# Host-laid-out inputs, an output stored turned and new engine orders in an attention and FFN kernel

## The reference

```python
x = L0_attn_resid_stream                         # (8, 256, 128) f32
xn = _layernorm(x, axis=-1)
x = x + _L0_attn_ref(xn, ...) + _L0_ffn_ref(xn, ...)
# attention, with a = _layernorm(xn, ln_w, ln_b)
q = einsum('bsd,hde->bshe', a, W_q) + b_q        # k, v alike
scores = where(causal, einsum('bqhe,bkhe->bhqk', q, k) * D_HEAD ** -0.5, -inf)
z = einsum('bhqk,bkhe->bqhe', softmax(scores, axis=-1), v)
attn_out = einsum('bqhe,hed->bqd', z, W_o) + b_o
# FFN
_quantize(W) = clip(round(W / (mean(abs(W)) + EPS)), -1.0, 1.0)
h = relu(einsum('bsd,fd->bsf', x, _quantize(W1)) + b1)
out = einsum('bsf,df->bsd', h, _quantize(W2)) + b2
```

## Time and profile before

| | |
|---|---|
| median of 3 runs (lowest, highest) | 269.41 us (269.0, 269.49) |
| profiled execution: its own time, its span | 270.71 us, 268.7 us |
| PE matmul busy | 259.7 us, 97% |
| PE weight load busy | 226.8 us, 84% |
| DVE busy | 233.4 us, 87% |
| ACT busy | 222.8 us, 83% |
| POOL busy | 212.0 us, 79% |
| granted TensorE clock | 1.000 throughout |

### The profile page before, as it was taken

How to read it: one execution, slowest core, us unless ns; L and a number is a source line. 1 busy time by engine, 2 the same in 40 slices (tenths; PEclk the granted TensorE clock), 3 DMA queues, 4 the chain that set the end, 5 groups by cost and what they waited for, 6 DMA issues and landing times.

```text
span 268.7 us, 7430 instructions
## 1 busy us (share of the span) xinstructions
PE 259.7 (97%) x2420; PEld 226.8 (84%) x2420; DVE 233.4 (87%) x1006; ACT 222.8 (83%) x798; POOL 212.0 (79%) x431
## 2 busy tenths in 40 slices
PE   6989899999999999999999999999999999999994
PEld 5767688799888998899897998889887998989874
DVE  2799999998999899997999899998999979997841
ACT  3589997988888997988978988889969889996950
POOL 5489999999859979599768979599786997576750
PEclk9999999999999999999999999999999999999999
DMA  7980000000000000000000000000000000000000
GB/s 166 257 206 1 1 2 4 0 1 2 22 1 2 0 23 1 4 0 2 20 4 4 0 2 20 4 2 2 20 2 1 2 1 22 0 4 0 22 2 20
DMA packets 12737, 5.72 MB, mean 21 GB/s; under 512 B 6790, under 2 KB 12444, under 8 KB 12700
## 3 DMA queue, kind: packets, MB, share of 16 engines
q1 hardware_dynamic: 12656, 5.25, 8.1%
q10 hardware_dynamic: 44, 0.01, 0.0%
HBM read 4.21 MB, written 1.05 MB: 20 GB/s over the span
## 4 chain that ended last, share of the span: by engine, by line
PE 87%; DVE 4%; POOL 3%; ACT 2%; DMA 1%; issue 0%; SPq 0%; POOLq 0%; ACTq 0%
PE m_ps L846 11%; PE s_ps L812 11%; PE m_ps L825 6%; PE m_ps L787 6%; PE m_ps L850 5%; PE m_ps L832 5%; PE m_ps L826 5%; PE m_ps L788 5%; PE m_ps L789 5%; PE s_ps L817 5%; PE m_ps L873 3%; PE m_ps L799 3%; PE m_ps L800 2%; PE m_ps L801 2%; DMA wq_raw<-in_L_attn_W_q 1%; PE m_ps L877 1%
## 5 line engine op out<-in xcount | busy, mean ns | idle before, releaser
L604 DVE CUSTOM_DVE_ANT_0 s_ps<-s_ps,causal 128x256 f32<-128x256 f32 (+1 forms) x256 | 84.8, 379 | 0.0
L465 ACT ACTIVATE prob<-s_ps,neg_max 128x256 f32<-128x256 f32 x128 | 65.4, 511 | 8.4 <-DVE neg_max L604 8.4
L384 POOL TENSOR_SCALAR prob<-prob,inv_sum 128x128 f32<-128x128 f32 x128 | 48.4, 378 | 24.1 <-DVE inv_sum L611 24.1
L386 POOL TENSOR_SCALAR prob<-prob,inv_sum 128x256 f32<-128x256 f32 x128 | 61.8, 483 | 0.0
L467 ACT ACTIVATE prob<-s_ps,neg_max 128x128 f32<-128x128 f32 x128 | 52.3, 409 | 0.0
L473 ACT ACTIVATE pT_wide<-m_ps 128x512 f32<-128x512 f32 x64 | 38.6, 606 | 16.2 <-PE m_ps L826 16.0
L377 POOL TENSOR_TENSOR qk_first<-k_all 128x128 f32<-128x128 f32 x64 | 29.1, 461 | 14.8 <-DVE k_all L592 14.7
L812 PE MATMUL s_ps<-k_all,q_last 64*128 64x256 f32 x384 | 39.2, 310 | 0.3 <-ACT prob L467 0.3
L846 PE MATMUL m_ps<-pT_wide,v 128*64 128x256 f32 x256 | 39.3, 385 | 0.0
L604 DVE DVE_READ_ACCUMULATOR2_ANT neg_max<- 128x1 f32 x256 | 36.2, 141 | 0.0
L812 PEld LDWEIGHTS s_ps<-k_all,q_last 64*128 64x128 f32 x384 | 26.9, 185 | 9.3 <-issue 7.7
...
## 6 DMA issues: line engine op xcount, KB each, us to landing
...
```

Of the source, the lines that this page charges most:

```text
L384: nc.gpsimd.tensor_scalar(prob[:, j, h, S:W], prob[:, j, h, S:W], inv_sum[:, j, 2 + h:3 + h], 0.0, ALU.mult, ALU.add)
L386: last = nc.gpsimd.tensor_scalar(prob[:, j, h, 0:S], prob[:, j, h, 0:S], inv_sum[:, j, h:h + 1], 0.0, ALU.mult, ALU.add)
L465: nc.scalar.activation(prob[:, j, h, 0:S], s_ps[:, pair % 2, h, 0:S], ACT.Exp, bias=neg_max[:, j, h:h + 1], scale=-1.0, accum_out=row_sum[ ...
L604: last = nc.vector.tensor_tensor_reduce(out=sc, in0=sc, in1=mask, scale=-SCALE, scalar=-MASKED, op0=ALU.add, op1=ALU.min, accum_out=neg_ma ...
```

## The change

The host now lays out what the kernel had to rearrange:

- W_q, W_k, W_v come as (128, 1024), feature by head and e, so a row is contiguous; W_o, W1 and W2 come as they lie in SBUF, W1 and W2 turned. Steps tf and cf are gone.
- All vectors of length 128 come as the columns of one (128, 24) array, loaded by one DMA on ACT's queue; L730, vc and vd are gone, as are five small DMAs on ACT's queue and two on SP's. POOL's bo (the sum of b_o and b2, L428) is now POOL's first step.
- The residual comes a second time, turned (8, 128, 256), into a tile with two slots, loaded two batches ahead by SP; DVE adds output bias and turned residual in one operation and the output is stored turned, from two slots. Steps ot, on PE and on DVE, are gone. The host turns the result back.
- The first halves of W_q and W_k are loaded, and split into high and low parts, in quarters of 256 columns; pr0 waits for the low parts of q and k one by one.
- The filler transposes are 12 and 5 instead of 4, 9 and 9.
- All twelve lists are new. The scores of pair 0 and the heads of duo 0 of the next batch are taken into the body's list; the body starts at tw4 of the batch before.

```diff
-BUSY = (4, 9, 9)
+BUSY = (12, 5)
+PARTS = [("q", slice(0, 2 * P)), ("k", slice(0, 2 * P)), ("q", slice(2 * P, 4 * P)), ("k", slice(2 * P, 4 * P)),
+         ("v", HALF[0]), ("q", HALF[1]), ("k", HALF[1]), ("v", HALF[1])]
-PE_HEAD = ("xa:3 xb:1 vd:1 pr0:2 pr1:0 pr2:3 xn:2 s0 pr3:0 s1 v0:2 v1:1 tf0:2 tf1:3 ta:0 s2 pr4:1 pr5:3 v2:2 s3 "
-           "tw0:0 pr6:1 pr7:2 f0:0 s4 tw1:3 v3:0 tn0:1 xh+:2 s5 f1:0 xn+:1 s6 tw2:3 pr0+:2 pr1+:1 s7 tw3:0 "
-           "pr2+:3 pr3+:2 tn1:1")
-PE_PLAN = ("z0-:0 z1-:1 s0 s1 tw4-:2 v0:3 tw5-:0 tn2-:1 tw6-:2 pr4:3 tw7-:0 tn3-:1 pr5:2 v1:0 s2 z2-:1 z3-:3 s3 "
-           "s4 tw0:2 v2:0 tw1:1 pr6:2 pr7:0 v3:1 oa-:3 f0:1 xh+:2 f1:0 s5 s6 tw2:2 tn0:1 xn+:0 ob- pr0+:2 pr1+:1 "
-           "ot-:0 tw3:3 s7 pr2+:2 pr3+:3 tn1:1")
+PE_HEAD = ("xa:0 xb:1 pr0:3 pr1:1 xn:3 pr2:2 pr3:1 s0 pr4:3 s1 ta:0 s2 v0:1 pr5:0 pr6:2 pr7:3 s3 s4 v1:1 v2:2 "
+           "v3:0 xh+:3 tw0:1 tw1:2 pr0+:3 f0:2 f1:1 s5 s6 tn0:2 pr1+:1 xn+:3 pr2+:2 pr3+:1 tw2:0 tw3:3 s7 s0+ "
+           "z0:0 tn1:2")
+PE_PLAN = ("tw4-:1 pr4:3 tn2-:2 z1-:1 s1 s2 tw5-:3 tw6-:2 tn3-:0 v0:1 tw7-:3 pr5:0 pr6:2 pr7:3 z2-:1 z3-:0 s3 s4 "
+           "v1:1 v2:2 v3:0 xh+:3 tw0:1 tw1:2 oa-:0 pr0+:3 f0:2 f1:1 s5 s6 tn0:2 pr1+:1 xn+:3 ob- pr2+:2 pr3+:1 "
+           "tw2:0 tw3:3 s7 s0+ z0:0 tn1:2")
+PE_TAIL = ("tw4-:3 pr4:1 tn2-:2 tw5-:3 z1-:0 s1 s2 tw6-:2 tn3-:0 pr5:1 tw7-:3 v0:0 pr6:2 pr7:3 v1:0 s3 z2-:1 "
+           "z3-:2 s4 s5 oa-:1 f0:2 ob- tw0:0 f1:2 tn0:3 tw1:1 s6 s7 tw2:2 tw3:0 tn1:3 v2:1 tw4:2 v3:0 tw5:3 z0:1 "
+           "z1:2 tw6:0 tn2:1 tn3:3 tw7:0 z2:1 z3:2 oa:3 ob")
...
+ACT_HEAD = ("wh0 wh1 wh2 xa wh3 wh4 pr0 pr1 xn pr2 pr3 aa wh5 e0 oh pr4 e1 e2 e3 pr5 pr6 pr7 e4 e5 e6 xh+ w0 e7")
+ACT_PLAN = ("w1- e8- e9- pr0 f0- f1- e10- pr1 e11- xn e12- pr2 e13- w2- w3- pr3 e14- z0- e15- w4- e0 pr4 e1 z1- "
+            "w5- w6- e2 e3 w7- pr5 pr6 pr7 e4 e5 z2- z3- e6 xh+ w0 e7")
...
+DVE_HEAD = ("lz nh wl0 wl1 wl2 xb wl3 xl pr0 pr1 xn pr2 pr3 m0 m1 th te0 te1 pr4 m2 i0 m3 m4 ln+ v0 pr5 m5 i1 pr6 "
+            "pr7 m6 i2 v1 v2 v3 m7 xh+ m8 m9 pr0+ m10 i3 m11 n0 m12 i4 pr1+ xn+ m13 pr2+ i5 i6 m14 m15 pr3+ m0+ "
+            "n1 z0 m1+ i7 n2 pr4+ z1 m2+ i0+ m3+ n3")
+DVE_PLAN = ("m4 ln+ v0 pr5 m5 i1 pr6 pr7 z2- m6 i2 z3- v1 v2 v3 m7 xh+ m8 m9 pr0+ m10 i3 m11 n0 m12 i4 pr1+ xn+ "
+            "o- m13 pr2+ i5 i6 m14 m15 pr3+ m0+ n1 z0 m1+ i7 n2 pr4+ z1 m2+ i0+ m3+ n3")
...
+POOL_HEAD = ("bo hs np vl0 g0 g1 k0 k1 k2 k3 vl1 ol p0 k4")
+POOL_PLAN = ("ln p1- xl k5- k6- p2- h0- k7- p3- k0 h1- k1 p4- p5- p6- k2 k3 p7- p0 k4")
+POOL_TAIL = ("ln p1- k5- k6- xl k7- p2- k0 p3- p4- k1 h0- p5- p6- k2 p7- k3 k4 h1- k5 p0 p1 p2 k6 p3 p4 k7 h0 p5 "
+             "h1 p6 p7")
...
             sp.dma_start(x_all[:, 0:TILES, :], x_v[:, 0:TILES, :]).then_inc(x_in[0], 16)
-            for n, w in (("q", w_q), ("k", w_k), ("v", w_v)):
-                load_half(n, w, 0)
+            for n in range(5):
+                load_weights(n)
             sp.dma_start(x_all[:, TILES:2 * TILES, :], x_v[:, TILES:2 * TILES, :]).then_inc(x_in[1], 16)
...
+            load_turned(0)
+            load_turned(1)
             for b in range(B):
-                sp.wait_ge(ot_done, b + 1)
-                sp.dma_start(out_v[b], out_sb[:, :, :]).then_inc(out_done, 16)
-            sp.wait_ge(out_done, 16 * B)
+                sp.wait_ge(o_done, b + 1)
+                sp.dma_start(outT[b], out_sb[:, b % 2, :]).then_inc(out_done[b % 2], 16)
+                if b + 2 < B:
+                    load_turned(b + 2)
...
+            act.dma_start(vecs[:, :], columns).then_inc(vec_in, 16)
...
                 wait(dve, o_psd, b + 1)
-                nc.vector.tensor_scalar(o_part[:, :], bank("oa", 0, b)[:, 0:S], out_bias[:, :], None, ALU.add).then_inc(o_done, 1)
+                dve.wait_ge(xT_in[b % 2], 16 * (b // 2 + 1))
+                wait(dve, out_done[b % 2], 16 * (b // 2))
+                nc.vector.scalar_tensor_tensor(out=out_sb[:, b % 2, :], in0=bank("oa", 0, b)[:, 0:S],
+                                               scalar=out_bias[:, :], in1=xT_cur[:, b % 2, :], op0=ALU.add, op1=ALU.add)\
+                    .then_inc(o_done, 1)
```

More of the change, by code:

```diff
@@ L51 @@
[L51 to L63, removed]
@@ new lines @@
+ACT_HEAD = ("wh0 wh1 wh2 xa wh3 wh4 pr0 pr1 xn pr2 pr3 aa wh5 e0 oh pr4 e1 e2 e3 pr5 pr6 pr7 e4 e5 e6 xh+ w0 e7")
+ACT_PLAN = ("w1- e8- e9- pr0 f0- f1- e10- pr1 e11- xn e12- pr2 e13- w2- w3- pr3 e14- z0- e15- w4- e0 pr4 e1 z1- "
+            "w5- w6- e2 e3 w7- pr5 pr6 pr7 e4 e5 z2- z3- e6 xh+ w0 e7")
+ACT_TAIL = ("w1- e8- e9- pr0 f0- f1- e10- pr1 xn e11- e12- pr2 e13- w2- pr3 w3- e14- e15- z0- w4- e0 pr4 e1 z1- "
+            "w5- e2 w6- w7- pr5 e3 pr6 e4 e5 e6 z2- e7 z3- e8 pr7 e9 e10 f0 e11 w0 f1 w1 w2 w3 e12 e13 w4 e14 e15 "
+            "z0 w5 z1 w6 w7 z2 z3")
@@ new lines @@
+DVE_HEAD = ("lz nh wl0 wl1 wl2 xb wl3 xl pr0 pr1 xn pr2 pr3 m0 m1 th te0 te1 pr4 m2 i0 m3 m4 ln+ v0 pr5 m5 i1 pr6 "
[3 more added lines that the diff above has]
+            "o- m13 pr2+ i5 i6 m14 m15 pr3+ m0+ n1 z0 m1+ i7 n2 pr4+ z1 m2+ i0+ m3+ n3")
+DVE_TAIL = ("m4 m5 v0 pr5 i1 pr6 m6 v1 m7 z2- i2 m8 m9 m10 z3- i3 pr7 i4 m11 o- n0 i5 m12 m13 n1 v2 m14 i6 m15 v3 "
+            "i7 z0 n2 z1 n3 z2 z3 o")
@@ L105, with attention_ffn_kernel @@
 BEFORE = before_it()
-def attention_ffn_kernel(nc, resid, attn_mask, w_q, w_k, w_v, w_o, b_q, b_k, b_v, b_o, ln_w, ln_b,
-                         w1, b1, w2, b2, out):
+def attention_ffn_kernel(nc, x, xT, w_q, w_k, w_v, w_o, w1T_in, w2T_in, columns, b_v, outT):
     ctx = ExitStack()
@@ L279, in _, with load_weights @@
         def _(sp):
[L280 to L285, removed]
+            x_v = x.rearrange("b (t p) d -> p (b t) d", p=P)
+            def load_weights(n):
+                name, cols = PARTS[n]
+                sp.dma_start(raw[name][:, cols], {"q": w_q, "k": w_k, "v": w_v}[name][:, cols]).then_inc(w_in[n], 16)
@@ L309, in _ @@
+            for n in range(2):
+                sp.wait_ge(out_done[n], 16 * B // 2)
         @block.gpsimd
@@ L779, in project @@
                     wait_low_input(b)
-                if b == 0 and pair < PAIRS // 2:
+                if b == 0 and 0 < pair < PAIRS // 2:
                     pe.wait_ge(w_lo_done, 2 + 2 * (pair // 2))
@@ L786, in project @@
                     dst = halves("pr", pair, b)[:, n, :]
+                    if b == 0 and pair == 0:
+                        pe.wait_ge(w_lo_done, n + 1)
                     nc.tensor.matmul(dst, wlo[kind][:, cols], x2T_hi[:, :], start=True, stop=False)
@@ L888, in last_output @@
                 last.then_inc(o_psd, 1)
-            def turn_output(b):
-                wait(pe, o_done, b + 1)
-                for t in range(TILES):
-                    last = nc.tensor.transpose(bank("ot", 0, b)[:, t * P:t * P + P], o_part[:, t * P:t * P + P], ident[:, :])
-                last.then_inc(ot_psd, 1)
             def turn_first_heads_input(kind):
@@ L916, in turn_hidden_input @@
                 last.then_inc(xn_psd, 1)
-            def turn_ffn(n):
-                pe.wait_ge(w12_in, 32)
-                for c in range(FC):
-                    src = w2_raw[:, c * P:c * P + P] if n else w1_raw[:, c, :]
-                    last = nc.tensor.transpose(bank("tf", n, 0)[:, c * P:c * P + P], src, ident[:, :])
-                last.then_inc(wT_psd, 1)
             def total_ffn():
@@ L970, with laid_out, by_input @@
         "L0_ffn_W1", "L0_ffn_b1", "L0_ffn_W2", "L0_ffn_b2"]
+def laid_out(x, _, w_q, w_k, w_v, w_o, b_q, b_k, b_v, b_o, ln_w, ln_b, w1, b1, w2, b2):
+    def by_input(w):
+        return w.transpose(1, 0, 2).reshape(D, H * E)
+    columns = np.stack([*b_q.reshape(PAIRS, P), *b_k.reshape(PAIRS, P), *b1.reshape(FC, P), ln_w, ln_b, b_o, b2], axis=1)
+    return {"x": x, "xT": x.transpose(0, 2, 1), "w_q": by_input(w_q), "w_k": by_input(w_k), "w_v": by_input(w_v),
+            "w_o": w_o.reshape(PAIRS, P, D).transpose(1, 0, 2).reshape(P, PAIRS * D), "w1T": w1.T,
+            "w2T": w2.T.reshape(FC, P, D).transpose(1, 0, 2).reshape(P, FC * D), "columns": columns,
+            "b_v": b_v.reshape(1, H * E)}
 def kernel(**inputs):
```

160 lines of the change are left out of this document (44 added, 116 removed).

## The result

The changed kernel takes 283.32 us (median of 4 runs, 282.79 to 283.79), the kernel before 269.45 beside it (269.00 to 270.02): a ratio of 1.0513, 95% interval 1.0482 to 1.0544. Its profiled execution took 283.72 us with a span of 281.8. The forecast was 269.8, the range 264.5 to 272.0: wrong.

A forecast was written before the change was run, and what follows sets the result against it. TensorE's stream bounds the body, and what feeds it the first batch. First batch 44.0 + six batches 184.4 + last batch 37.5 + waiting 0.2 + end 3.0 = 269.1 span, 269.8 us as a median; range 264.5 to 272.

The forecast's parts named there:

- Start: Before the first projection: turned input ready at 7.5 us, projection starting at 7.55 instead of 9.07, a gain of 1.5.
- the walk: First batch, followed step by step through the engines with start distances: PE leaves it at 44.4 us, taken as 44.0.
- Order of the first batch: First batch in the body's order with nothing ready: PE leaves it at 44.0 us, the least being 38.4.
- Period: Length of one batch in the body: 30.74 us instead of 31.01, bounds 30.5 to 30.9; six make 184.4.
- the output turn's 0.22: Every batch: two transposes of the output go from PE, saving 0.22 us.
- Last batch and end: Last batch 37.5 us plus 0.2 of waiting; behind the last matmul 3.0 instead of 4.05.
- the span plus 0.7: Whole kernel: the median of the runs was taken as the profiled span plus 0.7 us.
- A: Rival, first batch: it keeps its pace of 38.4 us, so the median is 264.2; chance 0.29.
- B: Rival, first batch: DVE's ternaries collide with POOL's wo_lo, losing up to 1.4 us, so 271.2; chance 0.20.
- the 1.49 row: Profile of the kernel before, near 8.25 us: a DVE subtraction took 1.49 us instead of 0.41 while POOL's wv_lo ran.
- C: Rival, body: the loop of DVE and ACT sets the period, 31.2 us, and all is 272.6; chance 0.11.
- D: Host's layout: changes nothing by itself, loads being hidden but for the first 5 us; part of the forecast, no separate chance.

The follow-up runs named there:

- e1: The changed kernel, with projection 0 of the first batch no longer waiting for the late halves of the weights: 276.48 us, ratio 1.0251.
- e2: e1 with POOL's wo_lo moved later in the first batch, away from DVE's ternaries: 275.45 us, ratio 1.0194.
- e9: e1 with POOL's first narrow keys ahead of the late halves, wo_lo and smaller steps moved, and PE's second scores ahead of a projection: 274.16 us, ratio 1.0185.
- e5: The changed kernel's layout and turned output without pair 0's late wait, but engine lists of the kernel before, less removed steps: 268.47 us, ratio 0.9953.

## Why the prediction was wrong

*The step that failed* is "Start", with its "x2T_lo at 7.5, pr0 at 7.55. Gain 1.5", and behind it the walk that begins with it. x2T_lo ended at 7.84, nearly as said; pr0 started at 14.32. I priced the waits that the change takes away from pr0 and never asked which waits are left once its condition is changed: pair 0 moved to the `elif`, and that waits for POOL. The walk then had DVE take pr0 at 9.55. That wait, which the prediction put at nothing, cost 6.8 us (e1).

*Order of the first batch*: 44.0 against 56.12, 12.1 too little. The runs split it, each by tw4 of one profiled execution, with the difference of the medians behind it: 6.8 the wait (e1; 6.8); 1.4 the collision with wo_lo (e2 against e1; 1.0, within the noise); 2.0 the late halves ahead of k0, pr4 ahead of s1 and the smaller moves beside them (e9 against e2, 48.00 to 46.03; 1.3). The last 2.0, to 44.0, no run isolates; e9 has at most half of it in its collision (1.53 for 0.48), and its clock was 0.59 and 0.73 from 15 to 25 us. I had walked DVE and ACT step by step and taken POOL, whose new list puts 3.8 us of late halves ahead of k0, as "close behind". That was the second fault: the walk checked POOL at its divisions, not at k0.

*Start, once the wait is gone*: 7.98 in e1 and 7.86 in e5, a gain of 1.1 to 1.2 for 1.5. The columns' DMA, for which I took nothing, did cost nothing: POOL waited 0.63 for it, had done bo by 2.97, and then waited 1.19 more for DVE. Its first rstd starts at 4.16 for 3.92 before, because DVE's statistics, which wait for the input's load, start at 3.11 for 2.87. And little of the gain reaches the body: with the old orders (e5) the whole first batch is about 0.2 shorter in the medians.

*Period*: 30.85 for 30.74, inside 30.5 to 30.9. The hole from s3 to s4 is gone (0.60 for 0.74). But the output turn's 0.22 is no saving by itself: with the old orders it buys nothing at all, since ACT sets the length from pr0 to pr3 there (e5). So what I summed term by term is one joint result of turn and orders.

*Last batch and end*: from 56.12 + 6 x 30.85 = 241.2 to the last matmul at 278.86 is 37.6 for 37.7; 3.0 for 3.0 behind it. Both right.

*From the span to the median.* The terms together are 12.7 too low (281.8 for 269.1); the other 0.8 of the 13.5 is the step "the span plus 0.7". It set the median of some executions against the span of another, slower one. The changed kernel's median is 1.5 above its profiled span, and a profiled execution's own time 1.9 above it (283.72 for 281.8).

*Rivals.* A is wrong: even with wait, late halves and wo_lo mended the new first batch is at 46.03, not 38.4. B happened, with 1.98 us for my 1.4 in the operation and 1.4 at tw4 (1.0 in the medians); I gave it 0.20 though the 1.49 row showed it beside POOL's like operation. C is wrong for the new orders: the period is 30.85 and not 31.2. D isn't contradicted: with the old orders the layout and the turned output together are 0.5% faster, but nearly all of that is the end, which the turned output shortens. About 0.2 us is left for the rest, no more than the noise.

The range had no case for the first batch above 46, while the walk was the least certain term. A term built from some 60 ordered steps deserved a bound of several us upward; a new order has many ways to be late and one to be on time.
